# A graph attention layer on one core: the product xG for two pairs at once, with 512 moving columns

## What is computed

```
output = x W;  q = x Wq;  k = x Wk
alpha  = relu(q kT) * (adj != 0)
alpha  = softmax(alpha, over the query rows)
y      = x + alpha output
result = (y - mean) / sqrt(var + 1e-5), per row
```

## Time and profile before

| | us |
|---|---|
| median of 3 runs | 530.29 (530.23 to 530.5) |
| the profiled execution | 531.49 |
| its span in the trace | 529.7 |
| PE busy | 520.2 |
| DVE, ACT, POOL busy | 387.6, 328.9, 285.7 |

### The profile page before, as it was taken

The page is one execution under the profiler, slowest core; times in us unless marked ns, Lnnn a source line. Parts: engine busy times, 40 slices in busy tenths (PEclk is TensorE's granted clock), DMA queues, the critical chain, the costliest instruction groups (busy, mean ns, idle before and its releaser), DMA issues.

```text
span 529.7 us, 10990 instructions
## 1 busy us (share of the span) xinstructions
PE 520.2 (98%) x3823; PEld 496.8 (94%) x3823; DVE 387.6 (73%) x724; ACT 328.9 (62%) x780; POOL 285.7 (54%) x212
## 2 busy tenths in 40 slices
PE   7999999999999999999999999999999999999995
PEld 5889999999999999999999999999999999999993
DVE  4766969497785958779496776949777695877657
ACT  5565485575657566665665666557575756766464
POOL 0387847384572838547283654728457373854002
PEclk9999999999999999999999999999999999999999
DMA  7504361522506133160523407052250614304022
GB/s 266 210 0 172 109 236 43 188 92 80 200 0 213 66 138 139 54 223 0 198 79 118 159 10 260 8 198 79 84 193 0 222 55 159 119 0 160 1 80 79
DMA packets 24243, 62.12 MB, mean 117 GB/s; under 512 B 1312, under 2 KB 2336, under 8 KB 22304
## 3 DMA queue, kind: packets, MB, share of 16 engines
q1 hardware_dynamic: 24224, 61.87, 32.7%
HBM read 45.09 MB, written 16.78 MB: 117 GB/s over the span
## 4 chain that ended last, share of the span: by engine, by line
PE 97%; DVE 1%; DMA 1%; issue 0%; POOLq 0%; POOL 0%; SPq 0%; ACT 0%; ACTq 0%
PE o_bank L238 12%; PE o_bank L239 12%; PE o_bank L240 12%; PE chain L238 11%; PE chain L240 11%; PE chain L239 11%; PE bank_y L238 6%; PE bank_y L240 6%; PE bank_y L239 6%; PE bank_z L240 3%; PE bank_z L238 3%; PE bank_z L239 3%; DMA xn<-in_w 1%; PE chain L369 0%; PE chain L375 0%; PE chain L374 0%
## 5 line engine op out<-in xcount | busy, mean ns | idle before, releaser
L960 POOL TENSOR_TENSOR s_lo<-xs,s_hi 128x512 fp32r<-128x512 f32 x60 | 89.5, 1520 | 101.3 <-ACT s_hi L495 101.3
L502 ACT COPY parts<-chain 128x256 f32<-128x256 f32 x180 | 66.9, 372 | 92.4 <-PE chain L240 91.1
L954 POOL TENSOR_TENSOR a_lo<-xt,a_hi 128x512 fp32r<-128x512 f32 x60 | 79.9, 1357 | 48.3 <-ACT a_hi L488 48.3
L240 PE MATMUL o_bank<-t_hi,a_lo 128*128 128x256 f32 x256 | 72.4, 283 | 0.0
L239 PE MATMUL o_bank<-t_lo,a_hi 128*128 128x256 f32 x256 | 72.4, 283 | 0.0
L238 PE MATMUL o_bank<-t_hi,a_hi 128*128 128x256 f32 x256 | 72.4, 283 | 0.0
L555 ACT ACTIVATE squares<-xn,neg_mean 128x512 f32<-128x512 f32 x64 | 46.3, 723 | 30.6 <-DVE neg_mean L756 26.0
L741 DVE SCALAR_TENSOR_TENSOR p_lo<-soft,inv_sum,p_hi 128x256 fp32r<-128x256 f32 x64 | 59.6, 948 | 3.0 <-ACT p_hi L545 3.0
L688 DVE TENSOR_TENSOR v_lo<-parts,v_hi 128x512 fp32r<-128x512 f32 x45 | 59.8, 1354 | 2.6 <-ACT v_hi L535 2.6
L524 ACT CAST t_hi<-parts 128x512 fp32r<-128x512 f32 x45 | 27.9, 621 | 47.0 <-DVE parts L703 38.9
L749 DVE SCALAR_TENSOR_TENSOR xn<-o_bank,xn 128x512 f32<-128x512 f32 x64 | 44.1, 690 | 10.5 <-PE o_bank L240 10.0
(11 more groups left out here) (171 smaller groups left out, 1727.7 us busy)
## 6 DMA issues: line engine op xcount, KB each, us to landing
xn<-in_x SPq DMA_DIRECT2D x16, 1024.0 KB, 5.2
xt<-in_x_t SPq DMA_DIRECT2D x15, 1024.0 KB, 4.8
out<-xn SPq DMA_DIRECT2D x15, 1024.0 KB, 4.2
adj<-in_adj_t SPq DMA_DIRECT2D x16, 512.0 KB, 3.4
xt<-in_x_t SPq DMA_DIRECT2D x4, 256.0 KB, 4.5
xn<-in_w SPq DMA_DIRECT2D x4, 256.0 KB, 4.7
xn<-in_wq_t SPq DMA_DIRECT2D x4, 256.0 KB, 5.9
parts<-in_wk_t SPq DMA_DIRECT2D x4, 256.0 KB, 5.9
```

The costliest lines, as they stand in the source:

```text
L240: return nc.tensor.matmul(dst, a[1], b[0], start=False, stop=last, skip_group_check=shared)
L502: nc.scalar.copy(dst[:, c], src[:, c]).then_inc(copied, 1)
L954: nc.gpsimd.tensor_tensor(a_lo[:, slot, a], xt[:, a], a_hi[:, slot, a].bitcast(F32), ALU.subtract).then_inc(a_lo_ready, 1)
L960: nc.gpsimd.tensor_tensor(s_lo[:, s], xs[:, s], s_hi[:, s].bitcast(F32), ALU.subtract).then_inc(s_lo_ready, 1)
```

## The change

A group i is now two pairs, a = 2i and b = 2i+1; z = 2i-1 and y = 2i-2 are the two before. PE's order for a group is

```diff
+            def fill_t(i):
...
+                copy_taken(2)
+                t_half(P6, 1, both)
+                copy_taken(3)
+                xs_split(S1)
+                t_half(P5, 0, both)
...
+            def fill_o_a(i):
+                for g in range(2):
+                    pe.wait_ge(p_lo_ready, 8 * i + M * g + M)
+                    pe.wait_ge(v_lo_ready, 8 * i + (V_AT[0][A12], 4)[g])
+                    for n in range(M):
+                        r = M * g + n
+                        if r in (0, 3):
+                            pe.wait_ge(added, 8 * i + (0 if r == 0 else 1))
+                        else:
+                            pe.wait_ge(masked, 4 * i + 2 + r)
+                        fill_row(r, o_bank[r % 3][:])
```

On ACT, `copy_t` of a half waits until DVE has split V's block in the same place, then for PE:

```diff
+            def copy_t(i, product, c):
+                block = {P1: A11, P6: A21, P5: A22}[product]
+                act.wait_ge(v_lo_ready, 8 * i - 4 + V_AT[1][block])
+                act.wait_ge(t_filled, HALVES * i + T_DONE[product, c])
+                nc.scalar.copy(parts[:, PART[product], c], chain[:, c]).then_inc(t_copied, 1)
```

The head of a group, and the stretch beside V of a, in ACT's order:

```diff
+                split_p(z, 0)
+                split_v(z, A22)
+                centred_squares(y, 0, 0)
+                split_v(z, A21)
+                copy_t(i, P1, 0)
+                split_s(i, 1, S2)
+                split_s(i, 1, S4)
+                copy_t(i, P1, 1)
+                split_s(i, 1, S1)
+                split_a(i, 1, A22)
+                split_p(z, 1)
+                split_p(z, 2)
+                copy_t(i, P6, 0)
...
+                copy_v(a, P5, 1)
+                split_p(a, 0)
+                split_a(i + 1, 0, A21)
+                split_p(a, 1)
+                split_v(a, A22)
+                split_s(i + 1, 0, S2)
+                split_s(i + 1, 0, S3)
+                split_s(i + 1, 0, S1)
+                split_v(a, A11)
...
```

The same two places in DVE's order, and in POOL's:

```diff
+                split_v(z, A11, V_AT[1])
+                sum_v(z, A21)
+                sum_t(i, A11, 0)
+                split_v(z, A22, V_AT[1])
+                split_p(z, 0)
+                sum_t(i, A11, 1)
+                split_p(z, 1)
+                split_p(z, 2)
+                split_v(z, A21, V_AT[1])
...
+                sum_v(a, A22)
+                split_p(a, 0)
+                sum_v(a, A11)
+                split_v(a, A22, V_AT[0])
+                split_p(a, 1)
+                split_v(a, A11, V_AT[0])
+                split_v(a, A12, V_AT[0])
+                sum_v(a, A21)
+                mask(b, 0)
+                split_p(a, 2)
+                split_p(a, 3)
+                split_v(a, A21, V_AT[0])
+                mask(b, 1)
+                residual(a, i, 0, 0)
```

```diff
+            def group(i, more=True):
+                split_s(i, 1, S2)
+                split_s(i, 1, S1)
+                split_s(i, 1, S4)
+                split_a(i, 1, A22)
+                reciprocal_root(2 * i - 2)
+                split_a(i, 1, A21)
+                if more:
+                    for s in (S3, S1, S2, S4):
+                        sum_x(i + 1, 0, s)
+                    split_a(i + 1, 0, A21)
+                    for s in (S2, S3, S1):
+                        split_s(i + 1, 0, s)
+                    split_a(i + 1, 0, A11)
+                    split_a(i + 1, 0, A12)
+                    split_s(i + 1, 0, S4)
+                    split_a(i + 1, 0, A22)
```

```diff
+            split_v(last, A21, V_LAST)
+            variances(last - 1)
             for r in range(R):
+                normalise(last - 1, 0, r)
+            for r in range(R):
+                residual(last, GROUPS - 1, 1, r, bank=bank_y[:, 0] if r == R - 1 else None)
```

More of the change, by code:

```diff
@@ L99, in gnn_resnorm @@
         minus_half = sb("minus_half", [P, R])
-        c1, c2, c3, c22, c11, c21 = (parts[:, i] for i in range(6))
+        C11, C21, C22 = range(3)
+        BLOCK_AT = {A11: C11, A21: C21, A22: C22}
         w_raw, wq_raw = xn[:, 1], xn[:, 0]
-        wk_raw = parts[:, 0:4].rearrange("q k j n -> q k (j n)")
+        wk_raw = parts[:, 0:2].rearrange("q i c j n -> q (i c) (j n)")
         wq_hi, wq_lo = t_hi, t_lo
@@ L176, in _ @@
         def _(sp):
[L177 to L185, removed]
+            READ_BY = {A11: S_SUMMED[S2], A12: S_SUMMED[S4], A21: S_SUMMED[S1], A22: S_SUMMED[S1]}
@@ new lines, in group @@
+            def group(i, first=False, more=True):
+                if first:
+                    sp.wait_ge(wt_lo_ready, 4)
+                else:
+                    sp.wait_ge(y_stored[1], 16 * i - 16)
+                load_xn(2 * i - 1, 1)
+                load_adj(2 * i)
+                if more:
+                    for u in (A11, A12, A22, A21):
+                        load_a(i + 1, u)
+                load_adj(2 * i + 1)
+                store(2 * i - 2, 0)
+                sp.wait_ge(y_stored[0], 16 * i)
+                load_xn(2 * i, 0)
+                if more:
+                    for u in (A21, A11, A12, A22):
+                        load_b(i + 1, u)
+                store(2 * i - 1, 1)
@@ L208, in _ @@
                 sp.dma_start(wk_raw[:, k], wk_rows[:, k]).then_inc(wk_loaded[k], 16)
-            load_xt(1, second=True)
-            load_adj(0, 0)
-            load_adj(1, 1)
+            sp.wait_ge(a_lo_ready[0], 4)
+            for u in range(4):
+                load_block(1, u)
+            sp.dma_start(adj[:], adj_t[0].rearrange("q (r n) -> q r n", r=R)).then_inc(adj_loaded, 16)
             sp.wait_ge(gt_lo_ready, 4)
             load_xn(0, 0)
[L215 to L227, removed]
+            sp.wait_ge(x_summed[1], 4)
+            sp.wait_ge(a_lo_ready[1], 4)
+            for u in range(4):
+                load_block(2, u)
+            load_adj(1)
+            for u in (A21, A11, A12, A22):
+                load_b(1, u)
+            group(1, first=True)
+            for i in range(2, GROUPS - 1):
+                group(i)
+            group(GROUPS - 1, more=False)
+            sp.wait_ge(y_stored[1], 16 * (GROUPS - 1))
+            load_xn(PAIRS - 1, 1)
+            store(PAIRS - 2, 0)
             for r in range(R):
@@ L714, in split_v, with sum_t @@
-            def split_v(p, u, at=V_AT):
+            ADDED = {A11: (P2, P1), A22: (P7, P5), A21: (P4, P6)}
+            COPIED = {P1: 0, P6: 2, P5: 4}
+            def sum_t(i, u, c, pairs=slice(0, 2)):
+                product, copied = ADDED[u]
+                dve.wait_ge(t_copied, COPIES * i + COPIED[copied] + c + 1)
+                dve.wait_ge(t_filled, HALVES * i + T_DONE[product, c])
+                part = parts[:, BLOCK_AT[u], c, pairs]
+                bank = bank_z[:, pairs] if u == A11 else bank_y[:, c, pairs]
+                nc.vector.tensor_tensor(part, part, bank, ALU.add).then_inc(t_summed, 1)
@@ L715, in split_v, with split_b @@
+            def split_v(p, u, at):
                 dve.wait_ge(v_hi_ready, 4 * p + at[u])
-                whole = {A22: c22, A11: c11, A12: chain_v, A21: c21}[u]
+                whole = chain_v if u == A12 else parts[:, BLOCK_AT[u], :, 0]
                 rows, j = slice(u // 2 * M, u // 2 * M + M), u % 2
                 rest(v_lo[:, rows, j], whole, v_hi[:, rows, j]).then_inc(v_lo_ready, 1)
-            def mask(p, slot, turn, g):
+            def split_b(i, u):
+                dve.wait_ge(a_hi_ready[1], 4 * i + A_HI[1][u])
+                rest(a_lo[:, 1, u], xt[:, u], a_hi[:, 1, u]).then_inc(b_lo_ready, 1)
@@ L899, in _ @@
             for g in range(2):
-                mask(0, 0, 0, g)
+                mask(0, g, first=True)
                 for r in range(g * M, (g + 1) * M):
@@ L903, in _ @@
             invert(0)
-            step(1, 1, 0)
-            step(2, 0, 1)
-            with dve.Fori(1, PAIRS // 2 - 1) as i:
-                step(2 * i + 1, 1, i)
-                step(2 * i + 2, 0, i + 1)
-            step(PAIRS - 1, 1, PAIRS // 2 - 1, more=False)
+            one = slice(1, 2)
+            sum_t(0, A11, 0, one)
+            split_p(0, 0)
+            sum_t(0, A11, 1, one)
+            for r in range(1, R):
+                split_p(0, r)
+            sum_t(0, A22, 0, one)
+            sum_t(0, A22, 1, one)
+            split_second_t(A11)
+            split_second_t(A22)
+            sum_t(0, A21, 0, one)
+            sum_t(0, A21, 1, one)
+            split_second_t(A12)
+            residual(0, 0, 0, 0)
+            residual(0, 0, 0, 1)
+            split_second_t(A21)
+            residual(0, 0, 0, 2)
+            residual(0, 0, 0, 3)
+            means(0, first=True)
+            for g in range(2):
+                mask(1, g)
+                for r in range(g * M, (g + 1) * M):
+                    relu_max(1, r)
+            split_b(1, A11)
+            sum_v(1, A22)
+            sum_v(1, A11)
+            split_b(1, A12)
+            invert(1)
+            split_v(1, A12, V_AT[1])
+            with dve.Fori(1, GROUPS - 1) as i:
+                group(i)
+            group(GROUPS - 1, more=False)
+            last = PAIRS - 1
             def mean_of(r):
```

(18 more changed lines are left out.)

962 lines of the change are left out of this document (589 added, 373 removed).

## The result

The changed kernel takes **540.5 us** (median of 6 runs, 538.45 to 541.73) against 530.3 for the kernel before (6 runs, 530.21 to 531.13): a ratio of 1.0178, interval 1.0156 to 1.0201. It is slower by 10.2 us.

A forecast was written before the change was run, and what follows sets the result against it. PE, busy 98% and never waiting in a steady pair, was taken as the bound. Columns -7.8, waits 7 x 1.6 and 6 x 1.1, end +2.4 gave +12.4 us: median 542.7 against 530.29, range 523 to 547.

The forecast's parts named there:

- T by 512 columns: In T, 84 matmuls of 512 columns replace 168 of 256: 1.12 us less in each of 7 groups, 7.8 in all.
- Wait 1: In T, PE waits before P5's first half for ACT's copy, behind DVE's V split delayed by POOL: 1.6 us, 7 groups.
- Wait 2: In a's output, PE waits before row 2 for DVE's mask, delayed beside POOL: 1.1 us in groups 1 to 6.
- Prologue: Work before the loop: claimed to be the same, so a change of 0.
- End: After the last V: residuals wait for DVE's normalising of pair 14, 2.4 us later.
- the collisions don't meet PE: Rival, chance 0.31: DVE's collisions with POOL don't delay PE; first wait 0 to 0.3, second 0; 527.0 us.
- half of it: Rival, chance 0.22: the two waits in T and a's output are only 0.8 and 0.5 us; 532.6 us.
- DVE did not become the bound: Denies a rival, chance 0.10: DVE bounds the group's head, adding 7 x 1.0 us; 549.7 us.
- The columns do buy their 1.12: Denies a rival, chance 0.02: T's wide matmuls save nothing, 0.240 us each; +7.8 on the forecast, 550 us.

The follow-up runs named there:

- e2_pool_short: Changed kernel with POOL's four low-part casts at the head of a group cut to 4 of 256 columns (work left out); 533.0 us, one run.
- e7_prologue: e6_all with ACT's copies of pair 1's P1 moved up, after the second exponent instead of the fourth; 523.86 us.
- e6_all: Changed kernel with the three edits of e1_head, e4_yield and e5_tail together; 524.48 us, ratio 0.9871 to the kernel before.
- e3_t256: Changed kernel with T's matmuls by 256 columns, two for each one of 512; 544.16 us, ratio 1.0248 to the kernel before.
- e1_head: Changed kernel with three DVE splits put ahead of T's first sum at the head of a group; 529.77 us, ratio 0.9983 to the kernel before.
- e4_yield: Changed kernel with one added POOL wait: next group's S4 low part waits for DVE's last V split of pair a; 536.34 us.
- e5_tail: Changed kernel with only the last step reordered, pair 14's squares and variances moved earlier; 538.51 us, ratio 1.0138 to the kernel before.

## Why the prediction was right

The forecast was 542.7 with slower at 0.59; it is 540.5. The two waits, the end and the columns are the terms that were forecast, and each was tried by an edit of its own; that the total came so near is luck in part, as the sum below shows. Step by step:

- **T by 512 columns, -7.8**: right. 0.2267 apart, and 62.76 - 61.64 = 1.12 a group once nothing waits. By the rule that was weighed against it (the Trainium skill, TensorE: Matmul & The Clock Gate, Back-to-back issue gap: N / 2.4 + 2.5 ns) it would be 0.21. The section gives that formula for the gap of an isolated matmul, and the prediction did not say so; for a stream of weight loads and matmuls, which this kernel is, the same section gives about 131 ns for a matmul of 512 columns. The trace agrees with neither: 226.7 ns at 512 columns and 120 at 256.
- **Wait 1, 1.6 a group**: 1.47, at the forecast place, by the forecast chain (PE, ACT's copy, DVE's split of V, POOL). Counted from T's start at 204.92 (P5's nominal place, 215.80, less 10.88), DVE's instructions end at 7.5, 8.9, 9.5, 10.7 and 11.35; forecast 7.5, 9.05, 9.7, 10.7 with 11.1, and 11.7. So the collisions of the two later `split_p` were worth less than I gave them. The split into collisions and order was off too: 0.90 and 0.57 instead of 1.3 and 0.3. With POOL's casts cut short (e2_pool_short) the ends are the forecast ones to 0.1, but 0.57 is left where I had 0.3: from ACT's copy (216.37 + 0.58) to PE (217.19) there is 0.24, and I had put 0.1, and the matmul behind the late one loses 0.08 more. The two errors nearly cancel.
- **Wait 2, 1.1 a group**: the right place and chain, but 0.46. From T's start, wait 1 taken off (206.39), the splits of A22, row 1 and A11 end at 39.5, 40.9 and 42.6; forecast 39.45, 41.05, 42.85. The mask of rows 0 and 1 then ends at 44.4 (44.8), weights 3 at 46.8 (47.3), A21 at 48.5 (49.1), the next mask at 49.1 (49.8). No single step is wrong: ten steps in one queue, most rounded up by some 0.1, made 0.7 against a wait that is the small difference of two large times.
- **Prologue, 0**: wrong, +1.0. I called it "the same work". It is, but not in the same order: before, ACT's copies of P1 stood between the exponents of pair 1, and after they stand behind all four. e7_prologue takes 0.8 of it back. The other 0.2, in pair 1's `xG`, was not tried; that stage takes 10.54 to 10.73 us in the profiles of the changed kernel and the experiments, which are alike there, against 10.34 in the one profile before.
- **End, +2.4**: +2.0. The variance came at 2.4 after V's end (forecast 2.6), the first residual at 5.5 (5.65) and the last at 8.7 (9.0): a mis-sized term, the mechanism as forecast.
- **The sum.** 11.2 + 6.6 + 2.4 - 7.8 forecast, 10.3 + 2.8 + 2.0 + 1.0 - 7.8 measured: 12.4 against 8.3. The median rose by 10.2. The 1.9 between are in no trace: the profiled execution lies 1.2 above its median before and 1.8 below it after, and 1.3 of these 3.0 are the later and the earlier start of pair 1's `xG` in the two profiles. What the other executions did is not recorded, so that the start makes up the 1.9 is a guess. The terms were 4.1 too high together, and the forecast missed the median by only 2.2 because of those unexplained 1.9: that part is luck.
- **The rivals.** That the collisions don't meet PE is wrong in both places. That half of it comes is right for wait 2 alone. DVE did not become the bound: e6_all has the same DVE work and no wait. The columns do buy their 1.12.

## What to carry to other kernels

When an engine's queue is paced by the slowest one (a sum that waits for a product), look whether ready work that others wait for can go in front of that instruction; three splits in another order were worth 10 us here, more than the 7.8 of the wider matmuls. A cost that is hidden at one order of the queues (DVE's splits beside POOL, 1.35 us each at no cost) is not hidden at the next: read such lengths out of the trace before the order is changed. And a matmul saving is not paid out while a wait behind it is measured from another engine: of 1.12 us a group, the first 0.48 went into a longer wait (e3_t256).

## What was unexpected of the hardware

- The collision costs both sides. Two of POOL's casts take 2.56 us together when DVE is out of the way (e1_head) and 3.00 when it is not; S4 takes 1.29 after e4_yield's pause and 1.47 without it, and the A22 behind it 1.29 and 1.73. So the 0.96 us for which POOL was held back cost it 0.40 only: that A22 ends 39.22 us after wait 1's late matmul (216.83 to 256.05) and ends 38.82 after it without the pause (217.19 to 256.01).
- Executions of one kernel differ by up to some 3 us: 538.45 to 541.73 for the changed kernel, and for the kernel before 530.21 to 531.13 in six runs but 530.04 to 533.50 in the nine that were timed beside e5_tail and e6_all. In the profiles the first V matmul starts between 5.12 (e5_tail) and 7.09 us (e3_t256), in code that no edit touches, and in e3_t256 the granted clock is 0.82 of full speed from 5 to 10 us and 0.84 from 10 to 15, where it is 1.00 in the profiles of the kernels before and after. Whether this is the whole scatter was not tried, and stays open.
